# TensorE order in a transformer-tower kernel: the sixth projection unit of a step goes ahead of the third score tile

## The chip, the cores and the metric

One core of one Trainium2 chip. The metric is device time in microseconds (us) for one execution of the whole program; lower is better. TensorE does matrix products into PSUM banks, VectorE (DVE), ScalarE (ACT) and GpSimd (POOL) work on tiles, SyncE (SP) issues most DMAs. The engines run their own instruction streams in program order and meet at semaphores.

## The reference, cut to what matters

```python
h = gelu(x[:, 1:] @ W_other + x[:, :1] @ W_read + b)        # 16 x 374 x 256
h = h + attention1(layernorm(h))      # cosine attention: softmax(sim) @ x, plus x
# attention 2 with routed heads, on x = layernorm(h), E = 8 experts, D = 128
m = router mask (16 x 374 x 8)
q = einsum('tc,ecd,te->td', x, q_proj, m)     # k and v likewise
scores = q @ k.T / sqrt(D), causal; attn = softmax(scores)
attn_out = attn @ v
final = einsum('td,edc,te->tc', attn_out, o_proj, m * routing_weights)
h = h + final
```

There are 16 sequences of 374 tokens, each handled as NT = 3 tiles of 128 tokens (the last has 118).

## The kernel before, in words

Every product is made of half-precision parts: a value is split into a high and a low f16 part, and `split_product` (L1820) issues three matmuls (high x high, high x low, low x high).

The 16 sequences pass through a software pipeline. One step works on several sequences at once: attention 1 of sequence `f`, the routed projections q, k, v of sequence `m` (one behind `f`), and attention 2 and the output product of sequence `n` (two behind `f`). The function `pipeline` calls `step` for steps 1 and 2 in full, then steps 3 to 14 in a hardware loop (12 trips), then the last two. The long branch of `step`, which the diff edits, is used by 14 steps: step 2, the 12 loop trips and step 15.

TensorE's order inside a step is written out by hand. `M(u, ...)` issues projection units: unit `u` is one expert of one projection, 6 matmuls of 374 columns. Units 0 to 7 make q from experts 0 to 7 in bank 0, units 8 to 15 make v in bank 5, 16 to 23 make k in bank 1. Each q unit waits until `mask_tokens` (DVE, L1407) has written `xm` for its expert. The step begins with `dots` (cosine products of attention 1) between units 0 to 3, then `score(n, 0)` and `score(n, 1)` into banks 2 and 3, unit 4, `turn_exp` (six transposes, L1871), `score(n, 2)`, unit 5, `attend` (27 matmuls, L1884 to L1888), units 6 and 7, a wait until all three tiles of attention 1's residual are written, and units 8 to 10.

`score(n, 2)` takes bank 2 again, so it waits until DVE has taken score 0 out of it:

```python
                if i == 2:
                    pe.wait_ge(s_scores_out, NT * n + 1)
```

The wait after units 6 and 7, which protects bank 5 (attention 1's first output tile lies there until it is read), counts all three tiles:

```python
                    M(6, 7)
                    pe.wait_ge(s_h2_ready, NT * (f + 1))
                    M(8, 9, 10)
```

DVE's order in the same stretch is: `exp_low` of tiles 0 and 1 (L1428) around `cosines`, `mask_tokens` for expert 5 (L1407), `mask_scores(n, 0)` and `mask_scores(n, 1)` (L1488: bank plus causal mask into `scores`, and the row maximum), `exp_low` of tile 2, `exp_lower` (two copies, L1437), `mask_scores(n, 2)`, `mask_tokens` for experts 6 and 7, then `residual` (L1445 and L1447, which signals `s_h2_ready` once a tile, with layer-norm sums between). ACT's `exp_scores` (L962 to L976) follows each `mask_scores`, and POOL's `low_probs` (L787) subtracts the high part of each tile of the probabilities from the full ones, both of them in SBUF. Later in the step ACT copies the head outputs `aoT` (L902) out of PSUM after `probs_v`, and then does `high_2` (L896) on what DVE's `norm_apply` (L1290) wrote.

Of the kernel before, what the change touches and what calls it, by code (L numbers as in the profile page):

```python
# [26 lines left out]
def audio_tower_kernel(nc, x, tok_w, tok_b, sim_matrix, gates, q_proj, k_proj, v_proj, o_proj, out):  # L27
# [19 lines left out]
    with ExitStack() as ctx:  # L47
# [135 lines left out]
        def as16(b, n):  # L183
            return b[:, 0:n // 2].bitcast(F16)
# [160 lines left out]
        def early(m):  # L345

            return isinstance(m, int) and m == 0

        def final(b):

            return isinstance(b, int) and b == B - 1
# [29 lines left out]
        def by_trip(b):  # L381

            return not isinstance(b, int) or b <= LAST_TRIP

        def later(b):

            return not isinstance(b, int) or b > 0
# [1331 lines left out]
        def _(pe):  # L1719
# [74 lines left out]
            def turn_rows(n, b, part, dst, done):  # L1794
                for c in range(NC):
                    for t in range(NT):
                        last = t_.transpose(as16(dst, NC * TP)[:, c * TP + t * P:c * TP + (t + 1) * P],
                                            xhl[n][:, part, c, t, :], ident16[:, :])
                last.then_inc(done, 1)
# [16 lines left out]
            def split_product(dst, left, right, starts, stops, done=None):  # L1816

                k = 0
                for lp, rp in ((0, 0), (0, 1), (1, 0)):
                    last = t_.matmul(dst, left[lp], right[rp], start=(starts and k == 0), stop=(stops and k == 2),  # L1820
                                     skip_group_check=True)
                    k += 1
                if done is not None:
                    last.then_inc(done, 1)

            def unit(m, which, e):

                done, slot = (s_q_done, s_k_done, s_v_done)[which], SLOT[which]
                if which == 0:
                    pe.wait_ge(s_xm_ready, E * m + e + 1)  # L1830
                if e == 0:
                    if early(m):
                        pe.wait_ge(s_w_lo, NC * (slot + 1))
                        pe.wait_ge((s_h_first, s_h_ready, s_h_ready)[slot], B)
                    if which == 0 and later(m):
                        pe.wait_ge(s_q_lo, m)
                    if which == 1 and later(m):
                        pe.wait_ge(s_k_lo, m)
                    if which == 2 and later(m):
                        pe.wait_ge(s_v_hi, m)  # L1840
                dst = qkv_bank[which][:, 0:T]
                for c in range(NC):
                    split_product(dst, [w_qkv[:, p, slot, c, e, :] for p in range(2)],
                                  [xm[:, e, p * NC + c, 0:T] for p in range(2)],
                                  e == 0 and c == 0, e == E - 1 and c == NC - 1,
                                  done if (e == E - 1 or which == 1 or which == 2 and not by_trip(m)) and c == NC - 1 else None)
# [17 lines left out]
            def turn_exp(f):  # L1864

                pe.wait_ge(s_exp1_lo, NT * f + NT - 1)
                k = 0
                for p in range(2):
                    for j in range(1, NT):
                        for i in range(j):  # L1870
                            last = t_.transpose(as16(turn[1], NC * TP)[:, k * P:(k + 1) * P],  # L1871
                                                exp1_hl[:, p, i, j * P:(j + 1) * P], ident16[:, :])
                            k += 1
                last.then_inc(s_exp1_turned, 1)
# [36 lines left out]
            def score(n, i):  # L1911
                if i == 0:
                    pe.wait_ge(s_q_lo, n + 1)
                    pe.wait_ge(s_k_lo, n + 1)
                    if later(n):
                        pe.wait_ge(s_pair_added, PAIRS * n)
                if i == 2:
                    pe.wait_ge(s_scores_out, NT * n + 1)
                split_product(out_bank[i % 2][:, 0:KEYS[i]], [qT[:, p, i * P:(i + 1) * P] for p in range(2)],
                              [kT[:, p, 0:KEYS[i]] for p in range(2)], True, True, s_scores_done)  # L1920
# [35 lines left out]
            def turn_probs(n):  # L1956
                turn_probs_low(n)
                turn_probs_high(n)
# [48 lines left out]
            def step(i, g1, f, m, n):  # L2007
                def F(fn, *a):
                    if f is not None:
                        fn(f, *a)  # L2010

                def M(*us):
                    if m is not None:
                        for u in us:
                            unit(m, SLOT[u // E] if by_trip(m) else u // E, u % E)

                def N(fn, *a):
                    if n is not None:
                        fn(n, *a)

                if final(n):
                    for p in range(E // 2):
                        pair(n, p)
                    weighted_sum(1, 0, 0, C)
                    weighted_sum(2, 0, 0, C // 2)
                    weighted_sum(2, 1, C // 2, C)
                    return
                if early(m):
                    M(*range(2))
                    pe.wait_ge(s_lo2, f + 1)  # L2030
                    turn_rows(1, f, 1, turn[1], s_turned2_lo)
                    M(*range(2, 7))
                    logits(f)
                    M(*range(7, 13))
                    turn_mask(f)
                    M(*range(13, 24))
                    return

                if f is not None and n is not None:
                    M(0)  # L2040
                    dots(f, 0)
                    M(1)
                    dots(f, 1)
                    M(2)
                    dots(f, 2)
                    M(3)
                    score(n, 0)
                    score(n, 1)
                    M(4)
                    turn_exp(f)  # L2050
                    score(n, 2)
                    M(5)
                    for t in range(NT):
                        attend(f, t)
                    M(6, 7)
                    pe.wait_ge(s_h2_ready, NT * (f + 1))
                    M(8, 9, 10)
                    probs_v(n)
                    M(11, 12)
                    pair(n, 0)  # L2060
                    pair(n, 1)
                    M(13)
                    pair(n, 2)
                    M(14)
                    logits(f)
                    pair(n, 3)
                    M(15, 16)
                    pair(n, 4)
                    M(17)
                    turn_mask(f)  # L2070
                    M(18)
                    pair(n, 5)
                    M(19)
                    pair(n, 6)
                    pair(n, 7)
                    for k in range(4):
                        M(20 + k)
                        pair(n, 8 + k)
                    return

                M(0, 1)
                score(n, 0)
                score(n, 1)
                M(2, 3)
                score(n, 2)
                pe.wait_ge(s_logits_out, B)
                pe.wait_ge(s_mask_row, B)
                turn_v(n)
                M(4, 5, 6, 7)
                turn_probs(n)  # L2090
                M(8, 9)
                probs_v(n)
                M(10, 11)
                pair(n, 0)
                pair(n, 1)
                M(12)
                pair(n, 2)
                M(13)
                pair(n, 3)
                M(14)  # L2100
                pair(n, 4)
                M(15)
                pair(n, 5)
                M(16)
                pair(n, 6)
                M(17)
                pair(n, 7)
                last_scores(m)
                M(*range(18, 24))
                pair(n, 8)  # L2110
                turn_probs(m)
                turn_v(m)
                pair(n, 9)
                probs_v(m)
                pair(n, 10)
                pair(n, 11)
# [59 lines left out]
            pe.wait_ge(s_mask_row, 1)  # L2176
            turn_rows(1, 1, 0, turn[0], s_turned2_hi)
            pipeline(pe, step)


# [23 lines left out]
```

## Time and profile before

| what | value |
|---|---|
| median of 3 runs | 697.69 us (697.32, 697.69, 700.32) |
| profiled execution, its own time | 699.35 us |
| span of the profiled execution, first to last instruction | 697.6 us |
| granted TensorE clock, mean | 0.998 |
| TensorE (PE) busy | 681.4 us, 98% |
| DVE busy | 546.7 us, 78% |
| POOL busy | 405.8 us, 58% |
| ACT busy | 345.4 us, 50% |

The profile is of one execution. A line number names a line of the kernel. PE is a matmul, PEld the load of its stationary operand. A row of the timeline can merge several like instructions (x6), its first number is the start and its second the length, both in us; the length of a matmul includes its way through the array, so that matmuls overlap and their starts tell the pace. Square brackets give idle time of the engine before the row, with what ended it.

### The profile page before, as it was taken

Reading aid. Unit: us, or ns where it says so; the run is one execution under the profiler, and the core shown is the slowest. Engines: PE = TensorE matmul, PEld = TensorE weight load, DVE = VectorE, ACT = ScalarE, POOL = GpSimd, SP = SyncE. Lnnn points to the kernel's source line nnn. Section 1 sums busy time; section 2 is a strip of 40 time slices with the busy share of each in tenths; the row PEclk is TensorE's granted clock in tenths of the full one; section 3 lists DMA queues with packets and bytes.
Section 4 is the critical chain, followed back from the end, with each engine's and each line's share of the span. In section 5 each row is a group of like instructions: output and inputs, shape, how many; then the busy total and the mean of one; then the engine's idle time right before and its main releaser. Section 6 shows DMA issues by size and latency. Waiting matters only on the chain.

```text
span 697.6 us, 17459 instructions
## 1 busy us (share of the span) xinstructions
PE 681.4 (98%) x4856; PEld 435.9 (62%) x4856; DVE 546.7 (78%) x1428; ACT 345.4 (50%) x768; POOL 405.8 (58%) x669
## 2 busy tenths in 40 slices
PE   9999989999999999999999999999999999999998
PEld 8887656565655656565655656565655656565555
DVE  5778868786979788796979788796979788786636
ACT  5977444444536354444636354444636354453443
POOL 7552325665747676565747676565747676563534
PEclk9999999999999999999999999999999999999999
DMA  9671142424324252423334242423334242422121
GB/s 247 161 183 50 62 103 43 107 53 90 69 50 112 49 117 49 103 54 87 67 53 112 49 117 46 106 54 86 66 55 112 49 117 45 107 57 68 24 75 31
DMA packets 128310, 57.29 MB, mean 82 GB/s; under 512 B 100264, under 2 KB 124056, under 8 KB 128152
## 3 DMA queue, kind: packets, MB, share of 16 engines
q1 hardware_dynamic: 127888, 56.60, 35.0%
q10 hardware_dynamic: 392, 0.32, 0.1%
q8 instruction: 15, 0.25, 0.1%
q14 instruction: 15, 0.12, 0.1%
HBM read 30.45 MB, written 9.01 MB: 57 GB/s over the span
## 4 chain that ended last, share of the span: by engine, by line
PE 81%; DVE 6%; issue 5%; POOL 3%; DMA 2%; ACT 2%; DVEq 0%; POOLq 0%; ACTq 0%; SPq 0%
PE bank L1820 70%; PE bank L1884 2%; PE bank L1888 2%; PE bank L1886 2%; DVE xm L1407 2%; PE bank L1740 2%; PE bank L1729 1%; DMA mask_all<-d_mask 1%; DMA xT<-xhl 1%; DVE region_b L1290 1%; DMA region_b<-in_x_dram 1%; DVE exp_hl L1428 1%; DVE region_a L1488 1%; POOL small L660 0%; DVE xinT L1211 0%
## 5 line engine op out<-in xcount | busy, mean ns | idle before, releaser
L1820 PE MATMUL bank<-xm,w_qkv 128*128 128x374 f16 x2304 | 409.6, 323 | 0.0
L1820 PEld LDWEIGHTS bank<-xm,w_qkv 128*128 128x128 f16 x2304 | 223.4, 98 | 146.8 <-issue 0.6
L1033 ACT ACTIVATE region_c<-bank,out_w 128x256 f32<-128x256 f32 x180 | 83.3, 473 | 159.1 <-PE bank L1820 142.4
L1820 PE MATMUL bank<-w_o,aoT 128*128 128x512 f16 x540 | 143.1, 379 | 0.4
L1407 DVE TENSOR_TENSOR xm<-xT,mask_all 128x1496 f16<-128x1496 f16 x128 | 139.5, 1103 | 1.5 <-DMA mask_all<-d_mask 1.3
L1312 DVE SCALAR_TENSOR_TENSOR h<-bank,out_w,h 128x256 f32 (+1 forms) x180 | 85.9, 477 | 47.5 <-ACT region_c L1033 45.2
L748 POOL TENSOR_TENSOR region_c<-region_c 128x512 f32<-128x512 f32 x46 | 68.7, 1493 | 25.4 <-ACT region_c L1033 20.5
L787 POOL TENSOR_TENSOR exp_hl<-exp,exp_hl 128x128 f16<-128x128 f32 (+2 forms) x48 | 50.5, 1053 | 56.4 <-ACT exp_hl L976 54.3
L1820 PEld LDWEIGHTS bank<-w_o,aoT 128*128 128x128 f16 x540 | 49.2, 98 | 51.4 <-DVE h L1312 12.9
L755 POOL TENSOR_TENSOR region_c<-region_c 128x256 f32<-128x256 f32 x46 | 47.6, 1034 | 5.8 <-POOL region_c L748 5.5
L902 ACT ACTIVATE aoT<-bank 128x374 f16<-128x374 f32 x15 | 7.2, 483 | 87.7 <-PE bank L1820 87.7
L762 POOL TENSOR_TENSOR h<-region_c,h 128x256 f32 (+1 forms) x45 | 41.2, 917 | 15.2 <-POOL region_c L755 15.2
L1290 DVE TENSOR_SCALAR region_b<-h,moments,small 128x256 f32 (+1 forms) x96 | 35.1, 410 | 12.4 <-POOL small L662 12.4
L926 ACT ACTIVATE region_a<-region_a,log_p,small 128x374 f32<-128x374 f32 (+2 forms) x48 | 28.3, 590 | 28.0 <-DVE region_a L1418 28.0
L1820 PE MATMUL bank<-xT 128*128 128x374 f16 (+2 forms) x288 | 38.4, 271 | 2.4 <-DMA xT<-xhl 2.4
L1884 PE MATMUL bank<-xh_sum,exp_hl 128*128 128x257 f16 x144 | 39.5, 274 | 0.0
L1888 PE MATMUL bank<-xh_sum,exp_hl 128*128 128x257 f16 x144 | 39.2, 272 | 0.0
L1886 PE MATMUL bank<-xhl,exp_hl 128*128 128x256 f16 x144 | 39.0, 271 | 0.0
L1740 PE MATMUL bank<-w_tok,xinT 128*128 128x256 f16 x288 | 37.6, 273 | 0.7 <-ACT h L865 0.7
L1273 DVE BATCH_NORM_STATS2 stats<-h 128x6 f32 (+1 forms) x96 | 35.8, 415 | 0.0
L725 POOL TENSOR_TENSOR lg<-lg 128x24 f32<-128x24 f32 x16 | 4.6, 287 | 52.8 <-DVE lg L1394 52.8
L1820 PEld LDWEIGHTS bank<-xT 128*128 128x128 f16 x288 | 25.4, 99 | 12.9 <-DMA xT<-xhl 2.8
(211 smaller groups left out, 1026.1 us busy)
## 6 DMA issues: line engine op xcount, KB each, us to landing
mask_all<-d_mask SPq DMA_DIRECT2D x32, 384.0 KB, 4.3
h<-in_x_dram SPq DMA_DIRECT2D x16, 256.0 KB, 4.9
out_dram<-h SPq DMA_DIRECT2D x31, 128.0 KB
rnorm_row<-d_rnorm SPq DMA_DIRECT2D x16, 192.0 KB, 3.6
d_v<-xinT SPq DMA_DIRECT2D x14, 192.0 KB, 4.4
xinT<-d_v SPq DMA_DIRECT2D x56, 48.0 KB, 2.3
h<-in_x_dram SPq DMA_DIRECT2D x15, 112.0 KB, 5.6
out_dram<-h SPq DMA_DIRECT2D x15, 112.0 KB
```

The lines of the kernel that those rows point to most:

```text
L748: g.tensor_tensor(prod_sum[:, 0:2, :], prod[:, buf, 0:2, :], prod[:, buf, 2:4, :], ALU.add).then_inc(s_tile_summed, 1)
L755: g.tensor_tensor(prod_sum[:, 2, :], prod_sum[:, 0, :], prod_sum[:, 1, :], ALU.add).then_inc(s_tile_summed, 1)
L787: done = g.tensor_tensor(probs_tile(1, i), full, probs_tile(0, i), ALU.subtract)
L1033: a.activation(prod[:, prod_buf(n, t), q, :], pair_bank(n, p)[:, C:2 * C], ACT.Copy, scale=weights_out(n)[:, t, 2 * q + 1:2 * q + 2]).then ...
L1290: v.tensor_scalar(xs[n][:, :, t, :], h[:, b, t, :].rearrange("p (c q) -> p c q", c=NC), moments[n][:, t, 0:1], small[n][:, 4, t:t + 1], AL ...
L1312: v.scalar_tensor_tensor(h[:, n, t, :], pair_bank(n, p)[:, 0:C], weights_out(n)[:, t, e0:e0 + 1], h[:, n, t, :], ALU.mult, ALU.add).then_i ...
L1407: v.tensor_tensor(xm[:, e, :, 0:T], xT[1][:, :, :, 0:T].rearrange("p a c t -> p (a c) t"), mask_all[:, e, 0:T].unsqueeze(1).broadcast_to([ ...
L1740: t_.matmul(projected(t), xinT[:, b % 2, xp, c, t * P:(t + 1) * P], w_tok[:, wp, c, :], start=(c == 0 and xp == 0 and wp == 0), stop=False ...
L1820: last = t_.matmul(dst, left[lp], right[rp], start=(starts and k == 0), stop=(stops and k == 2), skip_group_check=True)
L1884: t_.matmul(banks[t][:, 0:C + 1], high, xh_sum[:, j, 0:C + 1], start=(j == 0), stop=False, skip_group_check=True)
L1886: t_.matmul(banks[t][:, 0:C].rearrange("p (c q) -> p c q", c=NC), high, xhl[0][:, 1, :, j, :], start=False, stop=False, skip_group_check=True)
L1888: last = t_.matmul(banks[t][:, 0:C + 1], low, xh_sum[:, j, 0:C + 1], start=False, stop=(j == NT - 1), skip_group_check=True)
```

## The change

In the long branch of TensorE's `step`, the sixth projection unit, `M(5)`, and the third score, `score(n, 2)`, change places. Nothing is added or removed, no wait is edited, and no other engine's order changes.

```diff
                     score(n, 1)
                     M(4)
                     turn_exp(f)
+                    M(5)
                     score(n, 2)
-                    M(5)
                     for t in range(NT):
                         attend(f, t)
                     M(6, 7)
```

## Rows read from the trace of the kernel before

**Rows 1.** The page: busy us, share of the span and instructions of each engine.

```profile
PE 681.4 (98%) x4856; PEld 435.9 (62%) x4856; DVE 546.7 (78%) x1428; ACT 345.4 (50%) x768; POOL 405.8 (58%) x669
```

**Rows 2.** Waits of TensorE's matmuls: total us, times, longest us.

```profile
PE bank L1820 <- DVE row_max L1488: 7.5, 14, 0.6
```

**Rows 3.** Chain that ended last: start, us, what; first and last loop trip.

```profile
150.77 9.84 PE bank L1820 x63
...
583.03 9.84 PE bank L1820 x63
```

**Rows 4.** Timeline of PE, 223.7 to 234 us, one loop trip.

```profile
223.80 0.51 PE L1871 MATMUL bank<-ident,exp_hl 128*128 128x128 f16 x6
224.85 0.66 PE L1820 MATMUL bank<-kT,qT 128*128 128x384 f16 x3 [0.55 <-DVE row_max L1488]
225.35 1.11 PE L1820 MATMUL bank<-xm,w_qkv 128*128 128x374 f16 x6
226.30 0.27 PE L1884 MATMUL bank<-xh_sum,exp_hl 128*128 128x257 f16 x1
...
229.27 4.91 PE L1820 MATMUL bank<-xm,w_qkv 128*128 128x374 f16 x30
```

**Rows 5.** Timeline of DVE, 223.6 to 231 us, the same trip.

```profile
223.66 0.93 DVE L1407 TENSOR_TENSOR xm<-xT,mask_all 128x1496 f16<-128x1496 f16 x1
...
224.72 0.08 DVE L1488 DVE_READ_ACCUMULATOR2_ANT row_max<- 128x1 f32 x1
...
225.79 0.54 DVE L1488 CUSTOM_DVE_ANT_0 region_a<-bank,causal 128x384 f32<-128x384 f32 x1
...
226.26 0.93 DVE L1407 TENSOR_TENSOR xm<-xT,mask_all 128x1496 f16<-128x1496 f16 x1
227.11 1.16 DVE L1407 TENSOR_TENSOR xm<-xT,mask_all 128x1496 f16<-128x1496 f16 x1
...
230.22 0.48 DVE L1447 SCALAR_TENSOR_TENSOR h<-bank,inv_sum,region_b 118x256 f32 x1
```

**Rows 6.** Timeline of POOL and ACT, 226.2 to 228.8 us, the same trip.

```profile
226.28 1.19 POOL L787 TENSOR_TENSOR exp_hl<-exp,exp_hl 128x128 f16<-128x128 f32 x1 [2.81 <-ACT exp_hl L976]
227.50 1.30 POOL L787 TENSOR_TENSOR exp_hl<-exp,exp_hl 128x256 f16<-128x256 f32 x1
...
226.83 0.49 ACT L976 ACTIVATE exp_hl<-region_a,neg_max 128x256 f16<-128x256 f32 x1
227.23 0.28 ACT L962 ACTIVATE neg_max<-row_max,log_p 128x1 f32<-128x1 f32 x1
```

**Rows 7.** Timeline of POOL and DVE in step 2, 108 to 113 us.

```profile
108.13 0.43 POOL L787 TENSOR_TENSOR exp_hl<-exp,exp_hl 128x128 f16<-128x128 f32 x1 [13.59 <-ACT exp_hl L976]
109.35 0.83 POOL L787 TENSOR_TENSOR exp_hl<-exp,exp_hl 128x256 f16<-128x256 f32 x1 [0.79 <-ACT exp_hl L976]
...
108.24 0.56 DVE L1488 CUSTOM_DVE_ANT_0 region_a<-bank,causal 128x384 f32<-128x384 f32 x1
...
108.72 0.93 DVE L1407 TENSOR_TENSOR xm<-xT,mask_all 128x1496 f16<-128x1496 f16 x1
109.57 1.41 DVE L1407 TENSOR_TENSOR xm<-xT,mask_all 128x1496 f16<-128x1496 f16 x1
...
112.60 0.48 DVE L1447 SCALAR_TENSOR_TENSOR h<-bank,inv_sum,region_b 118x256 f32<-118x256 f32 x1
```

**Rows 8.** Timeline of PE in step 2, 107 to 115 us.

```profile
107.40 0.65 PE L1820 MATMUL bank<-kT,qT 128*128 128x384 f16 x3
...
111.81 3.33 PE L1820 MATMUL bank<-xm,w_qkv 128*128 128x374 f16 x20
```

**Rows 9.** Timeline of DVE and ACT, 233 to 237 us, the loop trip of rows 4.

```profile
233.67 1.06 DVE L1290 TENSOR_SCALAR region_b<-h,moments,small 128x256 f32 x3 [0.63 <-POOL small L662]
...
235.25 0.48 ACT L902 ACTIVATE aoT<-bank 128x374 f16<-128x374 f32 x1 [6.08 <-PE bank L1820]
235.63 0.83 ACT L896 ACTIVATE xhl<-region_b 128x768 f16<-128x768 f32 x1
```

## The prediction

> **What bounds the kernel now.** I read the page's busy shares first. TensorE is busy 681.4 us, 98% of the span, and DVE 78% [rows 1]: the reader is to see that TensorE sets the time, so that this change can only act through the few places where TensorE waits. Second, the chain that ended last: it is mostly TensorE, and the same piece of it, 63 matmuls in 9.84 us, comes back in each of the 12 loop trips [rows 3]. The first begins at 150.77, the last at 583.03, so a trip takes (583.03 - 150.77) / 11 = 39.30 us. Third, the table of TensorE's waits: the largest by far is the one for DVE's `row_max`, 7.5 us in 14 waits, one in each step that uses the edited branch [rows 2]. Fourth, the timeline of one trip around it [rows 4]: six transposes from 223.80, then nothing until `score(n, 2)` at 224.85 (0.55 us idle behind the last transpose's end), unit 5 from 225.35, `attend` from 226.30, and from 229.27 units 6 to 10 without a hole.
>
> **What the swap does to this wait.** Unit 5 needs `xm` of expert 5. DVE works in order: that `mask_tokens` runs from 223.66 to 224.59, and the row maximum for which the score waits ends at 224.80, 0.05 before the score starts [rows 4, 5]. With the same 0.05, unit 5 can start at 224.64. So the wait is not filled by unit 5; it is traded for a slightly shorter one, on `xm`. The saving is 224.85 - 224.64 = 0.21 us, no more. After it the lengths are those of the rows in the other order: unit 5 takes 226.30 - 225.35 = 0.95, the score 225.35 - 224.85 = 0.50. The score then starts at 225.59, its own wait long satisfied, and `attend` at 226.09 instead of 226.30. The transposes, and DVE's `exp_lower` behind them, don't move. If nothing followed, 14 steps less the second one (below) would give 13 x 0.21 = 2.7 us.
>
> **What it makes late.** The third score now comes 225.59 - 224.85 = 0.74 us later. Its last matmul ended at 224.85 + 0.66 = 225.51; it will end at 226.25. DVE took the tile at 225.79, 0.28 after that end, because it had its own work until then: there was slack. How fast DVE answers a semaphore when it has nothing else to do, these rows bound between the 0.05 seen from DVE to TensorE and the 0.28 seen here; I take 0.11, since a wait instruction of its own stands before `mask_scores`. It starts at 226.36, that is 0.57 late (0.51 to 0.74). Behind it in DVE's order are `mask_tokens` 6 and 7 and the whole residual.
>
> **A collision on top.** POOL's `low_probs` and DVE's `mask_tokens` don't overlap freely. In the trip, POOL's 128-column tile starts at 226.28, just as `mask_tokens` 6 starts (226.26 to 227.19), and takes 1.19 us, ending at 227.47; `mask_tokens` 7 then takes 1.16 instead of 0.93 [rows 5, 6]. In step 2, where the same POOL tile came while DVE was in `mask_scores`, it took 0.43; the 256-column tile came at 109.35, inside `mask_tokens` 6 (108.72 to 109.65), ended 0.53 after it, and `mask_tokens` 7 took 1.41 [rows 7]. I read: POOL is held until `mask_tokens` 6 ends, then goes first and holds `mask_tokens` 7 for its own run: 0.23 extra with the small tile, 1.41 - 0.93 = 0.48 with the larger. After the change the trip has the phase of step 2. POOL's small tile, still at 226.28, is done at 226.71, before `mask_tokens` 6, which runs 226.83 to 227.76. POOL's second tile follows ACT's row that ends at 227.32, as before, at 227.50 [rows 6]; that is inside `mask_tokens` 6. So `mask_tokens` 7 takes 1.41 instead of 1.16: 0.25 more. ACT itself isn't delayed: the third row maximum is ready at about 226.95, and ACT comes to it at 227.23 [rows 6].
>
> The Trainium skill ("SBUF — State Buffer", section "Who interferes with whom") says that a DVE instruction with two SBUF inputs and a GpSimd instruction that reads SBUF exclude each other, whole instruction by whole instruction, and that issue order decides who waits. By that rule too POOL's tile, issued before `mask_tokens` 7, goes first; it would also leave `mask_scores`, which has only one input in SBUF, alone. This case's 0.43 against 1.19 agrees, and if the two engines shared nothing the sum below would end at 699.6 instead.
>
> **Where it lands on TensorE.** The residual's last tile, which ended at 230.22 + 0.48 = 230.70, ends 0.57 + 0.25 = 0.82 late, at 231.52. TensorE counts all three tiles before unit 8. Thirty matmuls in 4.91 us, the last one's 0.32 deducted, are 0.158 each, so unit 8 started at 229.27 + 12 x 0.158 = 231.17 [rows 4]: the old slack was 0.42, with 0.05 for the semaphore. After the change TensorE arrives at 231.17 - 0.21 = 230.96 and is let go at 231.52 + 0.05 = 231.57. Net: 231.57 - 231.17 = **0.40 us later per loop trip**, although one wait became shorter.
>
> **Whether it stays lost.** Nothing after unit 8 gives it back, as ACT's work on the heads waits 6.08 us for TensorE's product, and what DVE, POOL and the mask transfer do later in the trip starts from TensorE's results. The delayed DVE work must not reach that point. `norm_apply` ended at 234.73 and will end at 235.55; ACT takes its result at 235.63, behind the head copy, and that moves to 236.03 with TensorE [rows 9]. Slack is 0.48, no further cost. SP's transposes of these rows start behind ACT, and move with TensorE.
>
> **First and last of the 14 steps.** In step 2 the score didn't wait (107.40, no idle) [rows 8], so nothing is saved. Its third `mask_scores` comes about 0.87 later (score at 107.40 + 0.95, ending 0.65 later, plus 0.11, against 108.24), but POOL's second tile then falls elsewhere and the 0.48 is spared, with up to 0.2 put back: 0.6 net. The residual's end 113.08 [rows 7] becomes 113.7, and unit 8 stood at 111.81 + 12 x 0.158 = 113.71 [rows 8]: 0 to 0.1. Step 15 lies between -0.2 (no stall) and 0.4; I take 0.1 for both steps together.
>
> **The sum.** 12 x 0.40 + 0.1 = 4.9 us. The profiled execution took 699.35 with a span of 697.6, and the median of the runs is 697.69; the difference is added to the median: **702.6 us**, 0.7% slower. What a measurement of this kernel can tell from no change is 0.5%, 3.5 us, so "same" ends at 701.2, which is 0.28 per trip.
>
> **Rivals.**
> - *Stall without the collision.* If `mask_tokens` 7 isn't stretched further (POOL's tile comes after `mask_tokens` 7 has begun), the residual is 0.57 late, unit 8 at 231.32: 0.15 per trip, 1.9 in all, 699.6. For it: POOL need come only 0.26 later against DVE. Against it: its start follows ACT, which isn't moved.
> - *The swap pays.* If the residual is under 0.42 late, TensorE isn't held longer than before, and under 0.21 late the whole 0.21 is kept: 13 x 0.21 = 2.7, 695.0. That needs DVE to win back 0.6 of 0.82, for instance by answering at once and `mask_tokens` 7 dropping to 0.93 (0.51 - 0.23 = 0.28 late, unit 8 at 231.03, a gain of 0.14 per trip, 696.0). That is the case if POOL's second tile lands behind `mask_tokens` 6. The rows put it 0.26 inside.
> - *The delay goes further.* If the 0.48 of slack at `norm_apply` is used up, by a POOL chain that is slowed in its new phase, ACT's next copy, the transposes and the router come later too: 0.2 more per trip, 0.60 x 12 + 0.1 = 7.3, 705.0.
> - *The swap does nothing for the wait.* Unit 5 held as long as the score was (0.05 more on the semaphore and DVE's drain) would cost 0.1 to 0.2 per trip more than my number: 704 to 705, with the rival before.
>
> **Chances and range.** The forecast 0.60; stall without the collision 0.16; the swap pays 0.09; the delay or the new wait costs more 0.12; other 0.03. Slower by over 0.5% comes from the forecast, except a tenth of it below 0.28 per trip, and from the costlier cases: 0.67. Same is that tenth, the case without the collision and most of the paying one: 0.28. Faster by over 0.5% needs over 3.5 us, more than the trade of waits allows, and only if most of the 7.5 us went would it come: 0.05. The range leaves out the paying case and the far end of the costly ones: 699.0 to 705.0.
>
> **What would show it.** In the profile of the changed kernel: TensorE's wait for `row_max` is gone; in its place one for `xm` of about 0.33 us idle, 13 times, before unit 5, and a new one for `h` (L1447) of about 0.45, some 12 times, before unit 8. POOL's first `low_probs` tile takes 0.43 in the loop, its second ends 0.53 after `mask_tokens` 6, and `mask_tokens` 7 takes 1.41. The 12 trips come at 39.70. The forecast is wrong if there is no wait for `h`, if `mask_tokens` 7 stays at 1.16 or less, or if the loop's period moves by another amount than unit 8 does against unit 5.

## The result, and the profile after

| | median us | runs | range |
|---|---|---|---|
| before, runs beside the changed kernel | 698.57 | 4 | 697.32 to 700.32 |
| changed | 705.26 | 4 | 704.62 to 707.02 |

The ratio is 1.0098, with a 95% interval of 1.0067 to 1.0129: the swap makes the kernel slower by about 6.8 us. The forecast was 702.6 us, with a range of 699.0 to 705.0. The direction and the mechanism were right; the difference that was forecast, 4.9 us, was over a quarter too small, and the range ended 0.26 us below the result.

The profiled execution of the changed kernel took 704.62 us, with a span of 702.9. TensorE's waits (total us, times, longest us), against [rows 2]:

```profile
PE bank L1820 <- DVE h L1447: 7.0, 14, 0.6
PE bank L1820 <- DVE xm L1407: 4.3, 13, 0.3
...
PE bank L1820 <- DMA pT<-exp_hl: 0.6, 1, 0.6
...
PE bank L1820 <- DVE row_max L1488: 0.2, 1, 0.2
```

Of the 7.5 us of waiting for `row_max`, the 7.0 us in 13 steps have gone; step 2 never had this wait, and the fourteenth of [rows 2] stands behind the loop, where 0.5 us were and 0.2 are left. 4.3 and 7.0 us have come for `xm` and for the residual `h`. The timeline of PE in the loop trip that answers to [rows 4]:

```profile
223.47 0.51 PE L1871 MATMUL bank<-ident,exp_hl 128*128 128x128 f16 x6
224.32 1.12 PE L1820 MATMUL bank<-xm,w_qkv 128*128 128x374 f16 x6 [0.34 <-DVE xm L1407]
225.28 0.65 PE L1820 MATMUL bank<-kT,qT 128*128 128x384 f16 x3
225.77 0.27 PE L1884 MATMUL bank<-xh_sum,exp_hl 128*128 128x257 f16 x1
...
228.74 2.06 PE L1820 MATMUL bank<-xm,w_qkv 128*128 128x374 f16 x12
231.35 2.87 PE L1820 MATMUL bank<-xm,w_qkv 128*128 128x374 f16 x17 [0.55 <-DVE h L1447]
```

Counted from the transposes' start (223.80 before, 223.47 now), unit 5 starts at 0.85, `attend` at 2.30 instead of 2.50, units 6 and 7 at 5.27 instead of 5.47. So far TensorE is 0.2 ahead. Then it stands: unit 8 starts at 7.88 instead of 7.37, 0.51 behind. DVE in the same trip, against [rows 5]:

```profile
223.34 0.92 DVE L1407 TENSOR_TENSOR xm<-xT,mask_all 128x1496 f16<-128x1496 f16 x1
...
226.12 0.56 DVE L1488 CUSTOM_DVE_ANT_0 region_a<-bank,causal 128x384 f32<-128x384 f32 x1 [0.58 <-PE bank L1820]
...
226.60 0.93 DVE L1407 TENSOR_TENSOR xm<-xT,mask_all 128x1496 f16<-128x1496 f16 x1
227.45 1.41 DVE L1407 TENSOR_TENSOR xm<-xT,mask_all 128x1496 f16<-128x1496 f16 x1
...
230.81 0.48 DVE L1447 SCALAR_TENSOR_TENSOR h<-bank,inv_sum,region_b 118x256 f32 x1
```

DVE now stands idle 0.58 us for the third score. `mask_tokens` 7, the second of the two later rows on `xm`, takes 1.41 us where it took 1.16, and the last residual tile ends at 231.29, 7.82 after the transposes' start instead of 6.90. POOL, against [rows 6]:

```profile
225.95 0.43 POOL L787 TENSOR_TENSOR exp_hl<-exp,exp_hl 128x128 f16<-128x128 f32 x1 [2.81 <-ACT exp_hl L976]
227.17 0.90 POOL L787 TENSOR_TENSOR exp_hl<-exp,exp_hl 128x256 f16<-128x256 f32 x1 [0.79 <-ACT exp_hl L976]
```

The small tile runs free in 0.43 us; the second comes at 227.17, inside `mask_tokens` 6 (226.60 to 227.53), and ends at 228.07, 0.54 behind it. Further down, against [rows 9], the delay is absorbed as forecast:

```profile
234.26 1.06 DVE L1290 TENSOR_SCALAR region_b<-h,moments,small 128x256 f32 x3 [0.64 <-POOL small L662]
...
235.44 0.48 ACT L902 ACTIVATE aoT<-bank 128x374 f16<-128x374 f32 x1 [6.60 <-PE bank L1820]
235.82 0.83 ACT L896 ACTIVATE xhl<-region_b 128x768 f16<-128x768 f32 x1
```

DVE's rows end at 235.32, half a microsecond before ACT takes them.

The measure used below is the loop's period: the start of the six transposes (L1871) in the second trip and in step 15, eleven trips apart. In the changed kernel these are

```profile
183.70 0.39 PE L1871 MATMUL bank<-ident,exp_hl 128*128 128x128 f16 x4
621.38 0.40 PE L1871 MATMUL bank<-ident,exp_hl 128*128 128x128 f16 x4
```

so (621.38 - 183.70) / 11 = 39.79 us a trip. In the kernel before the same two rows are

```profile
184.52 0.40 PE L1871 MATMUL bank<-ident,exp_hl 128*128 128x128 f16 x4
616.69 0.40 PE L1871 MATMUL bank<-ident,exp_hl 128*128 128x128 f16 x4
```

which gives 39.29.

### The profile page after: what moved, and what is told of

Read it like the earlier page. It is cut to its first block, busy times and chain, and to the rows that moved or that the text cites. A ratio compares the mean times of both kernels' runs of the same rounds, so it can differ in the third digit from the quotient of the medians.

```text
span 702.9 us, 17459 instructions
## 1 busy us (share of the span) xinstructions
PE 682.2 (97%) x4856; PEld 434.2 (62%) x4856; DVE 550.9 (78%) x1428; ACT 345.0 (49%) x768; POOL 402.9 (57%) x669
## 4 chain that ended last, share of the span: by engine, by line
PE 74%; DVE 12%; issue 6%; DMA 3%; ACT 2%; POOL 2%; DVEq 1%; SPq 0%; ACTq 0%; POOLq 0%
PE bank L1820 68%; DVE xm L1407 6%; PE bank L1740 3%; DVE h L1447 2%; DMA xT<-xhl 1%; PE bank L1729 1%; DVE stats L1273 1%; DMA pT<-exp_hl 1%; DMA mask_all<-d_mask 1%; DMA region_b<-in_x_dram 1%; DVE exp_hl L1428 1%; DVE inv_sum L1445 1%; DVE region_b L1290 0%; PE bank L1745 0%; PE bank L1908 0%
## 5 line engine op out<-in xcount | busy, mean ns | idle before, releaser
L1820 PEld LDWEIGHTS bank<-xm,w_qkv 128*128 128x128 f16 x2304 | 220.9, 98 | 161.4 <-DVE h L1447 12.3
L1407 DVE TENSOR_TENSOR xm<-xT,mask_all 128x1496 f16<-128x1496 f16 x128 | 143.1, 1132 | 0.6 <-DMA mask_all<-d_mask 0.5
L787 POOL TENSOR_TENSOR exp_hl<-exp,exp_hl 128x128 f16<-128x128 f32 (+2 forms) x48 | 38.6, 806 | 68.8 <-ACT exp_hl L976 68.8
L660 POOL TENSOR_TENSOR small<-small,m_half 128x3 f32<-128x3 f32 x32 | 36.2, 1133 | 5.9 <-POOL small L658 5.9
L658 POOL TENSOR_SCALAR small<-moments 128x3 f32<-128x3 f32 x32 | 7.8, 244 | 45.9 <-DVE moments L1282 45.8
```

Source lines behind the costliest of these rows:

```text
L1407: v.tensor_tensor(xm[:, e, :, 0:T], xT[1][:, :, :, 0:T].rearrange("p a c t -> p (a c) t"), mask_all[:, e, 0:T].unsqueeze(1).broadcast_to([ ...
```

## The experiments

Ratios are to the kernel before, run beside each on the same chip (its medians in the three groups of runs were 700.08, 699.78 and 699.96 us), with 95% intervals. "h ends" is the end of the last residual tile and "unit 8" the start of unit 8, both in us after the transposes' start, in a loop trip; between trips of one execution they differ by up to 0.02.

| kernel | ratio | transposes, trip 2 and step 15 | us per trip | h ends | unit 8 |
|---|---|---|---|---|---|
| before | 1 | 184.52, 616.69 | 39.29 | 6.90 | 7.37 |
| changed | 1.0098 (1.0067 to 1.0129) | 183.70, 621.38 | 39.79 | 7.82 | 7.88 |
| swap_fill | 0.9963 (0.9949 to 0.9976) | 186.03, 615.78 | 39.07 | 6.66 | 7.17 |
| swap_first | 1.0031 (1.0019 to 1.0043) | 184.26, 617.32 | 39.37 | 7.81 | 7.15 |
| swap_pool | 1.0036 (1.0024 to 1.0049) | 184.08, 616.46 | 39.31 | 7.34 | 7.40 |
| old_first | one run, 700.12 | 185.32, 617.35 | 39.28 | 6.91 | 7.37 |
| old_pool | one run, 701.75 | 186.46, 618.45 | 39.27 | 6.65 | 7.37 |
| swap_later | one run, 719.79 | 187.98, 635.00 | 40.64 | 8.66 | 8.72 |
| early_mask | 0.9939 (0.9920 to 0.9958) | 184.78, 615.12 | 39.12 | 7.13 | 7.20 |
| early_mask_first | 0.9922 (0.9903 to 0.9941) | 185.22, 613.23 | 38.91 | 7.13 | 7.01 |
| early_fill_first | 0.9937 (0.9918 to 0.9956) | 182.89, 611.00 | 38.92 | 6.79 | 7.01 |
| swap_again | 1.0087 (1.0067 to 1.0108) | 184.45, 622.38 | 39.81 | 7.81 | 7.88 |
| old_again | one run, 699.36 | 184.98, 617.02 | 39.28 | 6.91 | 7.37 |

**swap_fill: give DVE something to do until the late score is there.** In DVE's step of the changed kernel:

```diff
                     exp_lower(f)
+                    mask_tokens(m, E - 2)
                     mask_scores(n, 2, out_bank[0])
-                    mask_tokens(m, E - 2)
                     mask_tokens(m, E - 1)
```

> The changed kernel, and DVE does mask_tokens 6 before mask_scores(n, 2) instead of after it, so that it doesn't stand idle for the late score. My theory (the late third score pushes the residual, and unit 8 waits for the residual): DVE's row of copies is followed at once by mask_tokens 6, POOL's second tile comes inside mask_tokens 7 and holds nothing, the residual ends about 0.2 us earlier than in the kernel before, the wait of TensorE for h is gone, and only the 0.21 us saved at the score is left: loop trips of 39.08 us (39.30 before, 39.79 changed), ratio to the kernel before 0.996. Rival (unit 5 or the score itself is what costs, or the work downstream is slow for another reason): trips stay at 39.6 to 39.8, ratio 1.007 or more.

Both numbers came as expected: 39.07 us and 0.9963. DVE in one trip (transposes at 264.15):

```profile
265.79 0.41 DVE L1437 COPY exp_hl<-bank 128x512 f16<-128x512 f16 x1
266.13 0.92 DVE L1407 TENSOR_TENSOR xm<-xT,mask_all 128x1496 f16<-128x1496 f16 x1
266.97 0.54 DVE L1488 CUSTOM_DVE_ANT_0 region_a<-bank,causal 128x384 f32<-128x384 f32 x1
...
267.45 0.93 DVE L1407 TENSOR_TENSOR xm<-xT,mask_all 128x1496 f16<-128x1496 f16 x1
```

DVE has no idle time, and both `mask_tokens` take 0.93. TensorE's order is the changed one, untouched, and it is now faster than the old one by the 0.2 us that the trade of waits at the score is worth. So the swap on TensorE does not cost anything itself; what it does to DVE does.

**swap_first: wait before unit 8 for the first residual tile alone.**

```diff
                     M(6, 7)
-                    pe.wait_ge(s_h2_ready, NT * (f + 1))
+                    pe.wait_ge(s_h2_ready, NT * f + 1)
                     M(8, 9, 10)
```

> The changed kernel, and TensorE waits before unit 8 for the first residual tile alone (the one in bank 5) instead of all three. If the wait for h before unit 8 is the only place where the late residual hurts: trips of 39.08 us, ratio 0.996. My theory says the residual's delay of 0.92 us then arrives at the next place: norm_apply ends about 0.3 us too late for ACT's high_2, so SP's transposes and the router's logits come 0.2 to 0.3 us late, a wait for xT before the logits in the loop, trips of about 39.35 us, ratio 1.000 to 1.002. If the wait before unit 8 isn't the cause at all: trips stay at 39.79.

39.37 us a trip against the expected 39.35. The wait before unit 8 is gone, and 0.42 of the 0.50 us with it, but not the 0.7 that a removal of the only harm would give (39.79 to 39.08). ACT's copy `high_2` starts 0.15 us behind the end of the head copy instead of overlapping it, because DVE's `norm_apply` ends at 274.75, just before it:

```profile
274.16 0.48 ACT L902 ACTIVATE aoT<-bank 128x374 f16<-128x374 f32 x1 [5.88 <-PE bank L1820]
274.79 0.84 ACT L896 ACTIVATE xhl<-region_b 128x768 f16<-128x768 f32 x1
```

The place where TensorE pays was not the expected one. It is the product of pair 2, which waits for DVE's `h` of pair 0:

```profile
278.46 0.82 PE L1820 MATMUL bank<-w_o,aoT 128*128 128x512 f16 x3 [0.28 <-DVE h L1312]
```

DVE's `xhl` behind `high_2` (L1464), its `out_w` (L1509) and this `h` all come 0.25 to 0.27 us later after the transposes' start than in swap_fill, so it is the same delay, passed on. The wait that was expected, for `xT` before the logits in the loop, is not there.

The ratio, 1.0031 (2.2 us), is above the expected 1.000 to 1.002; the loop accounts for 12 x 0.08 = 1.0 us of it. The rest lies outside the loop, where TensorE stood 0.9 us for `pT` in step 15.

**swap_pool: keep POOL away from `mask_tokens` 6 and 7.** In `low_probs`:

```diff
                 for i in range(NT):
-                    pool.wait_ge(s_exp2_hi, NT * n + i + 1).then_inc(s_passed, 1)
+                    pool.wait_ge(s_exp2_hi, NT * n + (i + 1 if final(n) else NT)).then_inc(s_passed, 1)
```

> The changed kernel, and POOL starts low_probs only when all three tiles of the probabilities are there, so that it never runs beside mask_tokens 6 and 7. If POOL's second tile costs mask_tokens 7 its 0.48 us: mask_tokens 7 takes 0.93 instead of 1.41, the residual ends 0.48 earlier, the wait for h shrinks to 0.2 us, trips of 39.3 to 39.4 us, ratio 1.000 to 1.003 (the probabilities' second transpose comes some 0.6 us later and may cost up to 0.1). If POOL is innocent: mask_tokens 7 stays at 1.41, trips at 39.79, ratio 1.010.

39.31 us. The two `mask_tokens` rows together, and POOL's three tiles behind them:

```profile
265.84 1.78 DVE L1407 TENSOR_TENSOR xm<-xT,mask_all 128x1496 f16<-128x1496 f16 x2
```

```profile
267.83 1.93 POOL L787 TENSOR_TENSOR exp_hl<-exp,exp_hl 128x128 f16<-128x128 f32 x3 [5.46 <-ACT exp_hl L976]
```

1.78 instead of 2.26 us: 0.48 less, the residual ends 0.48 earlier, and the trip is 0.48 shorter. All of it arrives at TensorE. POOL's second tile was priced to the hundredth.

The ratio, 1.0036 (2.5 us), missed the expected 1.000 to 1.003, and the loop gives only 12 x 0.02 = 0.2 us of it. The rest is outside: 1.0 us of waiting for `pT` in step 15, and 1.1 us before the transposes of the probabilities (L1953) behind the loop. The second is a price of this edit: only swap_pool and old_pool have it.

**old_first and old_pool: the same two edits on the kernel before.**

> The kernel before with TensorE waiting before unit 8 for the first residual tile alone: the old order had 0.42 us of slack at this wait, so nothing changes: trips of 39.30 us. If the wait already bound the old kernel: shorter trips.

> The kernel before with POOL's low_probs held until all three probability tiles are there. mask_tokens 7 takes 0.93 us instead of 1.16 and the residual ends 0.23 us earlier, but the old order has 0.42 us of slack at unit 8, so the trips stay at 39.30 us.

39.28 and 39.27: no effect on the trip, though old_pool makes the residual end 0.25 us earlier. The old order's slack at unit 8 was real. (old_pool's one run, 701.75 us, is 2.0 us above the median beside it; 1.1 us of that are the stand before L1953.)

**swap_later: make the score later still.**

```diff
                     M(5)
+                    attend(f, 0)
                     score(n, 2)
-                    for t in range(NT):
+                    for t in range(1, NT):
                         attend(f, t)
```

> The changed kernel with the third score yet one attend tile later (1.0 us). If the time comes from the third score's lateness through the residual: mask_scores(n, 2) at 3.65 us behind the transposes' start instead of 2.65, the residual 0.5 to 0.7 us later than in the changed kernel (POOL's second tile falls before mask_tokens 6 and no longer stretches mask_tokens 7 by 0.48), trips of 40.3 to 40.5 us. If lateness of the score doesn't matter and something else in the swap costs: 39.8.

40.64, somewhat above the range. The score starts 1.33 us later than in the changed kernel, not 1.0, because `attend` now comes so early that it waits 0.3 for `exp_lower`'s copies; DVE stands idle 1.90 us, and the two `mask_tokens` again take 1.78 together. The residual ends 1.33 - 0.48 = 0.85 later, and so does the trip: 40.64 - 39.79 = 0.85. The one run's 719.79 us is 20.0 above the median beside it; 12 x 1.35 = 16.2 us are the trips, the rest lies outside the loop and was not followed up.

```profile
273.21 0.56 DVE L1488 CUSTOM_DVE_ANT_0 region_a<-bank,causal 128x384 f32<-128x384 f32 x1 [1.90 <-PE bank L1820]
...
273.69 1.78 DVE L1407 TENSOR_TENSOR xm<-xT,mask_all 128x1496 f16<-128x1496 f16 x2
```

**early_mask and early_mask_first: serve the wait instead of moving the waiter.** TensorE keeps the old order; on DVE

```diff
                     exp_low(f, 1)
-                    mask_tokens(m, E - 3)
                     mask_scores(n, 0, out_bank[0])
+                    mask_tokens(m, E - 3)
                     mask_scores(n, 1, out_bank[1])
```

and early_mask_first also has the weaker wait of swap_first.

> The same without the change of the wait before unit 8. ACT and POOL now start 0.65 us earlier too, POOL's second tile falls into mask_tokens 6 and mask_tokens 7 takes 1.41 us, not 1.16; the residual ends 0.25 us later than in the kernel before, and TensorE comes to its wait 0.38 earlier: a wait for h of some 0.2 us, trips of 39.1 us, ratio 0.996 to 0.997. If the collision with POOL is not there: no wait for h, trips of 38.92, as the kernel with the weaker wait.

> TensorE's old order; DVE does mask_scores(n, 0) before mask_tokens 5, so that the row maximum for which the third score waits comes 0.65 us earlier, and TensorE waits before unit 8 for the first residual tile alone. My theory: the third score starts right behind the transposes (0.33 us after them, not 1.05), unit 5 then waits 0.2 us for xm, attend starts when exp_lower is done, 0.38 us earlier than in the kernel before; nothing behind is late. Trips of 38.92 us (39.30 before), ratio 0.993 to 0.994. If the third score's wait is not worth its length: trips above 39.1.

39.12 and 38.91, both as expected. The ratio of early_mask, 0.9939, was not: 0.996 to 0.997 was expected, and 12 x 0.17 = 2.0 us are 0.3%. Three of its four executions had a mean granted clock of 1.000, but only one of the eleven of the kernel before beside it. At 1.000 the times are 695.60 (mean of three) and 698.35, at 0.998 they are 697.42 and 700.38 (mean of five): a ratio of 0.996 both times. In the second kernel, TensorE's rows around the score are

```profile
263.04 0.50 PE L1871 MATMUL bank<-ident,exp_hl 128*128 128x128 f16 x6
263.38 0.65 PE L1820 MATMUL bank<-kT,qT 128*128 128x384 f16 x3
264.08 1.12 PE L1820 MATMUL bank<-xm,w_qkv 128*128 128x374 f16 x6
265.15 0.28 PE L1884 MATMUL bank<-xh_sum,exp_hl 128*128 128x257 f16 x1
```

with the score right behind the transposes and `attend` at 2.11 us after their start instead of 2.50. In early_mask, POOL's second tile comes at 265.89, into `mask_tokens` 6, and `mask_tokens` 7 takes 1.40 as forecast:

```profile
266.32 1.40 DVE L1407 TENSOR_TENSOR xm<-xT,mask_all 128x1496 f16<-128x1496 f16 x1
```

That costs 0.2 us per trip before unit 8, which the weaker wait gives back. This 0.2 is not in TensorE's table of waits at all: the last matmul before unit 8 starts 0.35 us ahead of it instead of 0.158, and is itself counted as busy for 0.32 of them.

**early_fill_first: all three edits together.**

> TensorE's old order with the weaker wait before unit 8, and both reorderings of DVE: mask_scores(n, 0) before mask_tokens 5, and mask_tokens 6 before mask_scores(n, 2). The third score is in time in this order, so the second reordering has no stall to fill: trips of 38.91 us, as without it (38.91), ratio 0.992 to 0.994. If POOL's phase against mask_tokens mattered for TensorE even here: trips differ by 0.1 or more.

38.92, as without the second reordering. The two versions' ratios, 0.9922 and 0.9937, can't be told apart; early_mask_first has the fewer edits. Both beat the kernel before and the changed one.

**swap_again and old_again: what repeats.**

> The changed kernel itself once more, to see which parts of its loss repeat. If the late residual is the cause, 39.79 us per trip repeats exactly. The two smaller terms beside it, 0.27 us more in the first-to-second trip (the transposes of xT landing later) and 0.7 us before probs_v of step 15 (the transposes of pT landing later), repeat if the swap's order causes them, and change from one execution to the next if they are the queue's own variation. Ratio 1.008 to 1.012.

> The kernel before once more, for the same comparison: trips of 39.30 us, and between 0 and 0.5 us at the two places named for the changed kernel.

The trip repeats (39.81 and 39.28). TensorE's wait for the transposes of `pT` in step 15, seen in the changed kernel with 0.6 us, is there again:

```profile
PE bank L1820 <- DMA pT<-exp_hl: 0.4, 1, 0.4
```

It is there in all six profiles with the swapped order of TensorE (0.4 to 1.0 us), and of the seven with the old order only in early_mask_first (0.2): it goes with the swap.

The other term doesn't repeat: in the changed kernel the first-to-second trip took 0.3 us more than the later ones (143.65 to 183.70, 40.05), in swap_again nothing (144.65 to 184.45, 39.80), and in old_again the first trip took 40.48 (144.50 to 184.98), 1.2 us more than the later ones, with TensorE idle 1.0 us for `pT`, at a place where the kernel before had none. So single transfers in the first trips vary by up to a microsecond between executions of one program.

Not tried: letting DVE's third `mask_scores` carry its wait itself, instead of the separate wait instruction ahead of it, which would have measured how much of DVE's answering time is that instruction.

## Why the prediction was right and where it fell short

None of the three signs that the prediction named against itself came: the wait for `h` is there, `mask_tokens` 7 takes 1.41, and the period moved by 0.50 where unit 8 moved by 0.51.

**The trade of waits: right.** Unit 5 starts 0.85 us after the transposes began (forecast 0.84), with 0.34 idle before it (0.33), 13 times (13), and `attend` is 0.20 to 0.21 us early (0.21). swap_fill shows that this gain is real: it is all that is left when DVE is kept busy. One reading was off: the 14 waits for `row_max` are not one in each step of the edited branch, but 13 and one behind the loop; the sum counted 13 all the same.

**The collision with POOL: right, and shown.** 0.43, 0.54 behind `mask_tokens` 6, and 1.41 us are the forecast's numbers (0.43, 0.53, 1.41). swap_pool takes the collision away and gets 0.48 us of the trip back; early_mask produces it again in the old order of TensorE.

**Where it lands: right.** A new wait for `h` before unit 8, in all 14 steps, is the whole loss in the loop: swap_first removes it and 0.42 of the 0.50 us with it (the rest is a new wait further down), swap_later lengthens it one for one, old_first shows that it didn't bind before. Behind it nothing gave the time back, and `norm_apply` still had half a microsecond.

What failed were three sizes in the sum: DVE's answer to the late score (1.2 us over the trips), the first and the last of the 14 steps (1.0 us) and the base (0.9 us).

**The step that failed first is a term of the sum: how fast DVE answers.** "I take 0.11", the prediction said, between bounds of 0.05 and 0.28. The score's last matmul ends at 225.28 + 0.65 = 225.93 and DVE starts at 226.12: 0.19. The same 0.19 stands in swap_first, swap_pool, swap_later and swap_again. That is 0.08 of the 0.10 us per trip that were missing (0.50 lost, not 0.40); over 12 trips the 0.10 are 1.2 us. The bounds were right, the choice within them was not. With the upper bound, 0.28, the sum would have ended 12 x 0.17 = 2.0 us higher, at 704.6, still inside the range: this term alone doesn't put the result outside it.

**A second term: "I take 0.1 for both steps together" was too small by 1.0.** For step 2 the prediction said that "POOL's second tile then falls elsewhere and the 0.48 is spared". It wasn't:

```profile
107.69 1.44 POOL L787 TENSOR_TENSOR exp_hl<-exp,exp_hl 128x256 f16<-128x256 f32 x1 [0.79 <-ACT exp_hl L976]
...
107.66 2.26 DVE L1407 TENSOR_TENSOR xm<-xT,mask_all 128x1496 f16<-128x1496 f16 x2
```

```profile
112.08 1.12 PE L1820 MATMUL bank<-xm,w_qkv 128*128 128x374 f16 x6 [0.22 <-DVE h L1447]
```

The first fence is POOL and DVE in step 2 of the changed kernel, the second PE's unit 8. The tile arrived 0.03 us after `mask_tokens` 6 had begun, was held through all of it, and `mask_tokens` 6 and 7 took the same 2.26 us as in a loop trip; unit 8 stands 2.28 us behind the start of unit 6 (109.80) instead of 12 x 0.158 = 1.90, a loss of 0.38. The forecast took the phase of this single step from one execution, in which DVE and ACT were further ahead of TensorE than here: score 0's row maximum ended 0.26 us before the transposes' start there, and 0.10 behind it here. That lead was not the kernel's: in old_again, the same program as the kernel before, the row maximum ended 0.12 us behind, and POOL's second tile came 2.66 us after the transposes' start instead of 2.29. What sets the lead is not shown. Step 15 lost 0.2 at unit 8, inside the prediction's -0.2 to 0.4, and both executions of the changed kernel show 0.4 to 0.6 us more on `pT` there, which the prediction didn't have. Why the second transpose of `pT` lands later in that step after the swap is not shown.

**The sum as measured.** 12 x 0.50 for the trips, 0.38 for step 2, 0.2 and some 0.5 for step 15: 7.1 us, against ratios of 1.0098 and 1.0087, that is 6.8 and 6.1 us: a little over both, and inside both intervals.

**A third term: the base.** The difference was added to the median of three runs, 697.69. Beside the changed kernel it was 698.57, and of the 2.7 us between forecast and result this is 0.9. The range, read as a difference, went from 1.3 to 7.3 us, and the measured 6.7 lies inside it; so without the low base the time would have been inside too. Later medians of 9 to 20 runs were 699.78 to 700.08, so the base could be 2 us low.

**The rivals.** "Stall without the collision" falls with the 1.41; "the swap pays" falls with the wait for `h`; "the delay goes further" falls with the half microsecond left at `norm_apply`, though swap_first shows that it is near: without the wait before unit 8, it is what binds next. "The swap does nothing for the wait" falls with unit 5 at 0.85. The numbers of the last two, 705.0 and 704 to 705, come nearest to the result, but the mechanism of neither occurred.

## What to carry to other kernels

When a consumer on the critical engine is moved behind other work, follow what waits for its product: here a stand of 0.7 us behind the transposes was traded for one of 0.5, and the product came 0.74 us later to an engine that then idled and pushed its own queue into a wait with 0.42 us of slack. Before moving the waiter, look whether the releaser can be served earlier: one exchange of two DVE instructions took the same wait away and made the kernel 0.6% faster by the medians (0.4% at equal granted clock), 0.8% (0.7%) with a wait weakened to what it protects. And price a delay at the slack of the next wait that counts it, with the phase of the two engines that exclude each other worked out anew, since a shift of half a microsecond changes which instruction meets which.

## What the runs showed of the hardware

DVE took 0.19 us from the end of the score's last matmul, as the profile models it, to the start of the instruction behind a separate wait, where DVE to TensorE took 0.05 to 0.06 (`row_max` ends at 224.80 and the score starts at 224.85 before; `xm` ends at 224.26 and unit 5 starts at 224.32 after). How much of the 0.19 is the separate wait was not measured.

POOL's `low_probs` and DVE's `mask_tokens` exclude each other: the same 256-column tile took 0.67 us beside an idle DVE (swap_later), 0.90 when it came past the middle of `mask_tokens` 6 and 1.44 when it came at its start. The last two ended 0.54 behind `mask_tokens` 6, with the next `mask_tokens` stretched by 0.48. The Trainium skill ("SBUF — State Buffer", section "Who interferes with whom") describes an exclusive lock held for whole instructions between a DVE instruction with two SBUF inputs and a GpSimd instruction that reads SBUF; these runs agree with it.

TensorE's granted clock fell for about 3 us near 100 us in 7 of the 13 profiled executions and not in the other 6. The windows view of 98 to 104 us, of the kernel before and of the changed one:

```profile
98.00:104.00 6.00, 4.81 (x22) 2.86 (x23) 2.37 (x5) 1.44 (x3) 0.00 (x0) 0.72 0.32 56
```

```profile
98.00:104.00 6.00, 5.14 (x42) 3.63 (x43) 3.88 (x8) 2.50 (x5) 0.00 (x0) 1.00 0.26 42
```

The number before the last two is the clock: 0.72 is a mean of the 1.2 and 2.4 GHz levels, 1.00 the full one. It follows TensorE's wait for the transposes of `xT` there, 2.4 us in the kernel before, but old_again, the same program, kept 1.00 behind a wait of 2.8. The slow stretch is worth about 6 x (1 - 0.72) = 1.7 us. The 40 later executions of the kernel before agree: the 7 with a mean granted clock of 0.999 or 1.000 took 698.4 us on average, the 33 with 0.997 or 0.998 took 700.2. So two single profiles (spans of 697.6 and 702.9) can show a difference of 5.3 where the medians show 6.7: the loop's period is the safer measure.
